# Block transposes on VectorE and a trip through memory in place of TensorE transposes, for batches 4 to 7

## The chip, the cores and the metric

The kernel runs on one core of a Trainium2 chip. The metric is the device time of one execution, in microseconds; lower is better. Three runs of the kernel before gave 366.84, 367.55 and 368.38 us, a median of 367.55.

## What is computed

Eight batches of 512 rows with 512 features pass a gated channel attention over a context and then a gated, quantised feed-forward net (FFN). Only the second half matters here. Cut to that:

```python
def _quant_per_tensor(x):
    scale = max(max(abs(x)), 1e-6) / 127
    return round(x / scale), scale

def _qlinear(x2d, w, b):
    xq, sx = _quant_per_tensor(x2d)
    wq, sw = _quant_per_tensor(w)
    return (xq @ wq.T + b) * (sw * sx)

x = x + tanh(g_xattn) * attention(layernorm(x), ctx)
h = gelu(_qlinear(layernorm(x), w1, b1))       # 512 -> 2048
x = x + tanh(g_ffn) * _qlinear(h, w2, b2)      # 2048 -> 512
```

The scale of `h` is a maximum over all hidden values of all eight batches. So the second product can't begin before the last hidden value of the first is known.

## The kernel before, in words

The rows of a batch lie on 128 partitions, four rows to a partition (`NT` = 4 tiles of 128 rows), and stay in `X` for the whole kernel. The attention runs batch by batch up to about 140 us. From there to about 262 us comes the first FFN product, in eight **groups**, one per batch; after it the hidden values are scaled, rounded and multiplied by the second weights.

One group `g` does this:

- VectorE rounds the batch (`quantise_x`, L1010): four shifts of 128x512 (L1023) write integers into chunk 3 of a ring slot, and one cast (L1027) makes bf16 of them in the first half of chunk 2.
- TensorE turns the rounded rows with sixteen 128x128 transposes (`transposes`, L1389) into the two PSUM banks `psX`, so that features lie on partitions.
- VectorE copies them to `xqT` in `mid` with two copies (`evacuate`, L1033). `mid` has three slots, one for each of the ring's.
- TensorE computes 16 blocks of 128 hidden columns, four matmuls of 128x512 each (L1446), into six PSUM banks in rotation (`H_BANK`). Before each block it waits until ScalarE has emptied the bank (`gelu_done`).
- ScalarE applies GELU to each block (L689) and writes the group's 16 blocks into a slot of `ring`: three slots (`SLOTS`) of four chunks of 2048 columns.
- VectorE takes the maximum of each chunk (`group_max`, L1046; per block for the last two chunks of group 7, L1041).
- SP writes the chunks of groups 0 to 4 to memory (`spill`, L375); groups 5 to 7 stay in the ring.

No scheduler orders this. Each engine runs the groups one after another, and what stands before what is the order in which its `group` function is written. Two waits tie them. At a group's first block ScalarE waits for `hm_done` of `turn * (CH * SLOTS) + 1` (L683): `turn` is the group's number divided by three, so group 3 needs all maxima of groups 0 to 2, and group 6 those of groups 0 to 5. And it waits until the slot's last user is spilled. In VectorE's `group` (L1067) batch `g + 1` is rounded at the start of group `g`, after the last maximum of group `g - 1`, and copied out of PSUM between the second and the third maximum; TensorE does the transposes for it at block 12 of 16. Batches 1 and 2 are prepared elsewhere, amid the work on the second weights.

On GpSimd, the difference `T3` of two blocks of the second weights (L547) waits until the products of groups 0 to 5 are done, and `T2` (L550) until those of group 6 are; both go into slots of `mid` that are free by then.

## Time and profile before

| | |
|---|---|
| median of three runs | 367.55 us |
| the profiled execution | 368.52 us, span 366.7 us |
| busy over the span | TensorE 351.1 us (96%), VectorE 329.7 (90%), ScalarE 284.8 (78%), GpSimd 120.0 (33%) |
| stage of the first FFN product, 140 to 262 us | TensorE 119.81 busy of 122.00, VectorE 111.92, ScalarE 97.55, granted TensorE clock 1.00 |

Busy time is an average over stages. In this stage three engines take turns at being waited for, so it is read from the timelines of each, and from what ended each wait. A row of a timeline gives start, length, engine, line, operation, result and operand, the number of instructions merged, and in brackets the idle time ahead of it with what ended it. Operations of one engine overlap a little, so start-to-start times are shorter than durations. Matmul ends are modelled.

### The profile page before, as it was taken

How to read it: one execution, taken by the hardware profiler on the slowest of the kernel's cores; microseconds unless marked ns; L12 is line 12 of the kernel's file. 1: busy time of each engine (PE TensorE's matmuls, PEld its weight loads, DVE VectorE, ACT ScalarE, POOL GpSimd, SP SyncE). 2: the span in 40 equal slices, each digit the busy share in tenths (PEclk: the TensorE clock that was granted, in tenths of full speed). 3: DMA queues.
4: the chain of work that ended last, by engine and by line, in shares of the span. 5: the costliest groups of instructions: out<-in, count | busy, mean ns of one | idle time of the engine just before them, and what ended most of it. 6: DMA issues, size and time to landing. Idle time of an engine off the chain costs nothing.

```text
span 366.7 us, 6639 instructions
## 1 busy us (share of the span) xinstructions
PE 351.1 (96%) x2403; PEld 242.1 (66%) x2416; DVE 329.7 (90%) x630; ACT 284.8 (78%) x493; POOL 120.0 (33%) x178
## 2 busy tenths in 40 slices
PE   8799989999999989999999999999999999999995
PEld 2755767887886875554535445454548888888884
DVE  3489899999999978999999988987769999999996
ACT  1465879889886975879859988789799999999620
POOL 2544578778779791069000000431000000000000
PEclk9699999999999999999999999999999999999999
DMA  7999978566302463858748760000191999995225
GB/s 225 372 405 403 400 282 268 195 233 224 117 9 108 124 220 132 330 243 331 292 165 343 317 260 0 1 2 0 44 415 58 388 395 425 424 422 228 102 116 229
DMA packets 22963, 84.78 MB, mean 231 GB/s; under 512 B 2129, under 2 KB 11857, under 8 KB 14482
## 3 DMA queue, kind: packets, MB, share of 16 engines
q1 hardware_dynamic: 22272, 83.89, 59.3%
q10 hardware_dynamic: 658, 0.46, 0.5%
q8 instruction: 19, 0.31, 0.3%
q14 instruction: 14, 0.11, 0.1%
HBM read 54.99 MB, written 29.36 MB: 230 GB/s over the span
## 4 chain that ended last, share of the span: by engine, by line
PE 59%; DVE 19%; ACT 9%; POOL 5%; issue 5%; DMA 2%; DVEq 0%; SPq 0%; ACTq 0%; POOLq 0%
PE PS L1491 19%; PE PS L1446 17%; PE PS L1266 7%; DVE hmax L1046 6%; PE PS L1327 6%; ACT ring L709 5%; DVE hmax L839 2%; PE PS L1308 2%; PE PS L1275 2%; DVE ring L1023 2%; PE PS L1287 2%; POOL ring L493 2%; DMA X<-in_x 2%; POOL w1q L495 1%; PE PS L1298 1%
## 5 line engine op out<-in xcount | busy, mean ns | idle before, releaser
L689 ACT ACTIVATE ring<-PS,bias,sc 128x512 f32<-128x512 f32 x128 | 96.4, 784 | 22.4 <-DVE hmax L1046 6.8
L1446 PE MATMUL PS<-mid,w1q 128*128 128x512 bf16 x489 | 108.5, 379 | 1.2 <-ACT ring L689 0.3
L1446 PEld LDWEIGHTS PS<-mid,w1q 128*128 128x128 bf16 x500 | 48.4, 98 | 58.4 <-ACT ring L689 1.5
L1046 DVE TENSOR_REDUCE hmax<-ring 128x1 f32<-128x2048 f32 x30 | 67.5, 2281 | 5.6 <-ACT ring L689 5.6
L709 ACT ACTIVATE ring<-ring,sc 128x2048 int16<-128x2048 f32 x29 | 55.6, 1991 | 0.0
L1491 PE MATMUL PS<-w2q,ring 128*128 128x256 f16 x336 | 39.0, 273 | 0.0
L1174 DVE SCALAR_TENSOR_TENSOR X<-PS,sc,X 128x512 f32<-128x512 f32 x48 | 36.1, 766 | 0.0
L1491 PEld LDWEIGHTS PS<-w2q,ring 128*128 128x128 f16 x336 | 32.9, 98 | 4.0
L1266 PE MATMUL PS<-ring 128*128 128x129 f32 x256 | 33.0, 291 | 0.9 <-ACT ring L612 0.9
L1327 PEld LDWEIGHTS PS<-w2q,ring 128*128 128x128 f32 x256 | 29.2, 192 | 6.7 <-issue 6.7
L1266 PEld LDWEIGHTS PS<-ring 128*128 128x128 f32 x256 | 32.1, 207 | 2.1 <-issue 2.1
L1327 PE MATMUL PS<-w2q,ring 128*128 128x128 f32 x256 | 30.5, 277 | 0.4 <-DVE w2q L879 0.4
L621 ACT ACTIVATE ring<-mid,small 128x128 f32<-128x128 f32 x64 | 24.9, 404 | 4.8 <-DVE small L805 4.8
L1491 PE MATMUL PS<-mid,w1q 128*128 128x256 f16 x224 | 26.7, 273 | 0.3 <-DVE X L1174 0.3
L759 DVE BATCH_NORM_STATS2 small<-X 128x6 f32<-128x512 f32 x32 | 20.0, 682 | 7.0 <-DMA X<-in_x 7.0
L886 DVE SCALAR_TENSOR_TENSOR X<-PS,X 128x512 f32<-128x512 f32 x32 | 21.6, 689 | 3.5 <-PE PS L1327 3.4
L1491 PEld LDWEIGHTS PS<-mid,w1q 128*128 128x128 f16 x224 | 21.7, 98 | 3.4 <-issue 0.9
L612 ACT ACTIVATE ring<-X,small 128x512 f32<-128x512 f32 x28 | 20.7, 819 | 4.0 <-POOL small L449 4.0
L577 ACT ACTIVATE ring<-X,small 128x512 f32<-128x512 f32 x32 | 22.9, 716 | 0.5
L547 POOL TENSOR_TENSOR mid<-w2q 128x2048 f16<-128x2048 f16 x1 | 4.1, 4072 | 55.6 <-PE PS L1446 55.6
L727 ACT ACTIVATE w1q<-ring 128x2048 f16<-128x2048 int16 x7 | 13.3, 1902 | 9.2 <-PE PS L1491 9.2
L1167 DVE TENSOR_TENSOR X<-X,small 128x1024 f32<-128x1024 f32 x16 | 19.8, 1235 | 0.1
(151 smaller groups left out, 591.7 us busy)
## 6 DMA issues: line engine op xcount, KB each, us to landing
spilled_hidden<-ring SPq DMA_DIRECT2D x20, 1024.0 KB, 3.9
ring<-spilled_hidden SPq DMA_DIRECT2D x20, 1024.0 KB, 9.3
ring<-in_ctxT SPq DMA_DIRECT2D x8, 1024.0 KB, 5.5
ring<-in_ctx SPq DMA_DIRECT2D x8, 896.0 KB, 8.2
X<-in_x SPq DMA_DIRECT2D x7, 1024.0 KB, 9.5
out<-X SPq DMA_DIRECT2D x7, 1024.0 KB, 9.9
ring<-in_w1T SPq DMA_DIRECT2D x4, 1024.0 KB, 13.4
ring<-in_w2T SPq DMA_DIRECT2D x8, 512.0 KB, 3.5
```

The lines of the kernel that those rows point to most:

```text
L577: nc.scalar.activation(out[:, i, :], X[:, b, i, :], ACT.Square, bias=nmean[:, t:t + 1], accum_out=ssq[:, t:t + 1]).then_inc(sq_done, 1)
L612: nc.scalar.activation(q_sb[b % 2][:, i].rearrange("p h d -> p (h d)"), X[:, b, i, :], ACT.Identity, scale=rstd1[:, i:i + 1], bias=nmr1[:, ...
L621: nc.scalar.activation(E_sb[:, j, :], S_sb[:, j, :], ACT.Exp, scale=-1.0, bias=nb[:, j:j + 1], accum_out=Z[:, j:j + 1]).then_inc(exp_done, 1)
L689: nc.scalar.activation(ring[:, s * CH + c, (h % CH) * N:(h % CH + 1) * N], PS[:, hidden_bank(s, h), :], ACT.Gelu, scale=SC1, bias=bias1[:, ...
L709: nc.scalar.activation(ring16[:, s * CH + c, 0:CW], ring[:, s * CH + c, :], ACT.Copy, scale=ISH).then_inc(hy_done, n)
L886: V.scalar_tensor_tensor(X[:, b, i, :], PS[:, OUT_BANK[i], :], 1.0, X[:, b, i, :], ALU.mult, ALU.add, accum_out=sums[:, 4 * b + i:4 * b + ...
L1046: V.tensor_reduce(hmax[:, bass.ds(CH * g + c, 1)], ring[:, s * CH + c, :], AX.X, ALU.max, apply_absolute_value=True).then_inc(hm_done, 1)
L1174: V.scalar_tensor_tensor(x, sums_of(p, bank), SC2, x, ALU.mult, ALU.add).then_inc(added, 1)
L1266: mm = nc.tensor.matmul(PS[:, h // 2, h % 2 * (P + 1):h % 2 * (P + 1) + P + 1], q_sb[b % 2][:, i, h, :], k_sb[b % 2][:, i, h // 2, first:f ...
L1327: mm = nc.tensor.matmul(PS[:, OUT_BANK[i], h * P:(h + 1) * P], cT_sb[b % 2][:, h, i, :], M_sb[b % 2][:, h, :], start=False, stop=(h == NH ...
L1446: mm = nc.tensor.matmul(PS[:, hidden_bank(s, h), :], w1v[:, k, h * P:(h + 1) * P], xqT[:, s, k, :], start=(k == 0), stop=(k == NH - 1))
L1491: mm = nc.tensor.matmul(sums_of(p, bank)[:, j], left[:, k, j * P:(j + 1) * P], right[:, k, :], start=(start and k == 0 and (j == 0 or (p, ...
```

## The change

For batches 4 to 7 (`CARRIED` = 4 and up) TensorE's transposes and VectorE's copies from PSUM are gone. VectorE still rounds the rows. Then it turns them within 32x32 blocks, four instructions of 128x512 bf16 into the second half of chunk 2 (`turn_x`). SP writes the 512 KB to memory (`write_rows`) and reads them back with four DMAs, each of which gathers one of four 32-feature groups into its 32 partitions of `mid` (`fetch_rows`). There the columns of a batch no longer lie in one run: TensorE's moving operand is a view in runs of 32 numbers (`turned_block`). For these batches rounding and turning of batch `g + 2` stand in group `g`, between its second and its third maximum, in place of batch `g + 1`'s rounding at the group's start.

```diff
--- before.py
+++ after.py
@@ -46,6 +46,7 @@
     out_v = out.rearrange("b (p i) d -> b p i d", i=NT)
     w1_v = w1T.rearrange("(k p) (a n) -> p k a n", p=P, a=PIECES // NH)
     w2_v = w2T.rearrange("(q k p) n -> q p k n", p=P, q=PIECES)
+    carry = nc.dram_tensor("carried_rows", (B, NT, 32, NT, D), BF16, kind="Internal").ap()
     spill = nc.dram_tensor("spilled_hidden", (SPILLED * CH, P, CW), F32, kind="Internal").ap()
 
     with ExitStack() as es:
@@ -122,6 +123,21 @@
         bpt = mid[:, 1536:2048]
         S_sb = mid[:, 2048:3072].rearrange("p (j e) -> p j e", e=P)
         xqT = mid[:, :].bitcast(BF16).rearrange("p (s k n) -> p s k n", s=SLOTS, k=NH)
+        xqB = mid[:, :].bitcast(BF16).rearrange("p (s t m) -> p s t m", s=SLOTS, t=NT)
+        CARRIED = SLOTS + 1
+
+        def turned_block(g, k):
+
+            return xqB[:, g % SLOTS].rearrange("p t (k i w) -> p k i t w", k=NH, i=NT)[:, k]
+
+        def rounded_rows(g):
+
+            return ring[:, g % SLOTS * CH + 2, 0:CW // 2].bitcast(BF16)
+
+        def turned_rows(g):
+
+            return ring[:, g % SLOTS * CH + 2, CW // 2:CW].bitcast(BF16)
+
         ring16 = ring[:, :, :].bitcast(I16)
         hq = w1q[:, :].bitcast(F16).rearrange("p (c k n) -> p c k n", c=CH, n=N)
         blocks_h = w1q[:, :].bitcast(F16).rearrange("p (c k n) -> p c k n", c=CH, n=HN)
@@ -199,6 +215,9 @@
         w2_step, w2y_done, w2q_done = (sem(n) for n in ("w2_step", "w2y_done", "w2q_done"))
         xs_step, xs_pow, scales = (sem(n) for n in ("xs_step", "xs_pow", "scales"))
         y_done, xq_done, xT_done, xqT_done = (sem(n) for n in ("y_done", "xq_done", "xT_done", "xqT_done"))
+        turned_x = sem("turned_x")
+        written = [sem(f"written{g}") for g in range(B)]
+        moved = [sem(f"moved{g}") for g in range(B)]
         h_done, gelu_done, hm_done = (sem(n) for n in ("h_done", "gelu_done", "hm_done"))
         spilled = [sem(f"spilled{s}") for s in range(SLOTS)]
         back_in = [[sem(f"back_in{s}_{c}") for c in range(CH)] for s in range(SLOTS)]
@@ -369,10 +388,31 @@
                 load_w2(q)
 
 
+            def write_rows(g):
+
+                sp.wait_ge(turned_x, NT * (g - CARRIED + 1))
+                sp.dma_start(carry[g].rearrange("t r a m -> (t r) a m"),
+                             turned_rows(g).rearrange("p (a m) -> p a m", a=NT)).then_inc(written[g], 16)
+
+            def fetch_rows(g):
+
+                sp.wait_ge(written[g], 16)
+                sp.wait_ge(h_done, KH * (g - SLOTS + 1))
+                for a in range(NT):
+                    sp.dma_start(xqB[32 * a:32 * a + 32, g % SLOTS],
+                                 carry[g].rearrange("t r a m -> a r t m")[a]).then_inc(moved[g], 16)
+
             for g in range(SPILLED):
                 for c in range(CH):
                     sp.wait_ge(gelu_done, KH * g + (c + 1) * KH // CH + len(H_BANK))
                     sp.dma_start(spill[g * CH + c], ring[:, (g % SLOTS) * CH + c, :]).then_inc(spilled[g % SLOTS], 16)
+                    if c == 0 and g > 2:
+                        fetch_rows(g + 1)
+                if g >= 2:
+                    write_rows(g + 2)
+            fetch_rows(SPILLED + 1)
+            write_rows(B - 1)
+            fetch_rows(B - 1)
 
             for p in range(B):
                 if p + SLOTS < B:
@@ -1026,6 +1066,14 @@
                 dve.wait_ge(y_done, 4 * g + 4)
                 V.tensor_copy(xq, yt.rearrange("p i d -> p (i d)")).then_inc(xq_done, 4)
 
+            def turn_x(g):
+
+                dve.wait_ge(xq_done, 4 * g)
+                rows = rounded_rows(g).rearrange("p (i k a w) -> p i k a w", i=NT, k=NH, w=32)
+                out = turned_rows(g).rearrange("p (a k i w) -> p i k a w", a=NT, k=NH, w=32)
+                for i in range(NT):
+                    V.transpose(out[:, i], rows[:, i]).then_inc(turned_x, 1)
+
             def evacuate(g, s):
 
                 dve.wait_ge(xT_done, g + 1)
@@ -1065,14 +1113,17 @@
             V.reciprocal(ISW2, SW2).then_inc(w2_step, 1)
 
             def group(g, s, turn, last):
-                if g > 1 and not last:
+                if g == 2:
                     quantise_x(g + 1, (s + 1) % SLOTS, turn + (s + 1) // SLOTS)
                 group_max(g, s, 0)
                 group_max(g, s, 1)
                 if g == 0:
                     evacuate(2, 2)
-                if g > 1 and not last:
+                if g == 2:
                     evacuate(g + 1, (s + 1) % SLOTS)
+                if 2 <= g < B - 2:
+                    quantise_x(g + 2, (s + 2) % SLOTS, turn + (s + 2) // SLOTS)
+                    turn_x(g + 2)
                 group_max(g, s, 2)
                 group_max(g, s, 3)
 
@@ -1435,16 +1486,22 @@
                         pe.wait_ge(xqT_done, 3)
                         pe.wait_ge(w2_step, 5)
                         across(4, W2MAX).then_inc(w2_all, 1)
-                    if h == (KH // 2 if g == 0 else KH // 4 if g == 1 else 3 * KH // 4) and not last:
+                    if h == (KH // 2 if g == 0 else KH // 4 if g == 1 else 3 * KH // 4) and g + 1 < CARRIED:
                         if g == 1:
                             pe.wait_ge(w2_step, 6)
                         transposes(g + 1, (s + 1) % SLOTS)
                     pe.wait_ge(gelu_done, KH * g + h + 1)
                     for k in range(NH):
-                        if h == 0 and k % 2 == 0:
+                        if h == 0 and k % 2 == 0 and g < CARRIED:
                             pe.wait_ge(xqT_done, 2 * g + k // 2)
-                        mm = nc.tensor.matmul(PS[:, hidden_bank(s, h), :], w1v[:, k, h * P:(h + 1) * P], xqT[:, s, k, :],
-                                              start=(k == 0), stop=(k == NH - 1))
+                        if h == 0 and k == 0 and g >= CARRIED:
+                            pe.wait_ge(moved[g], 16 * NT)
+                        hidden, w = PS[:, hidden_bank(s, h), :], w1v[:, k, h * P:(h + 1) * P]
+                        if g < CARRIED:
+                            mm = nc.tensor.matmul(hidden, w, xqT[:, s, k, :], start=(k == 0), stop=(k == NH - 1))
+                        else:
+                            mm = nc.tensor.matmul(hidden.rearrange("p (i t w) -> p i t w", i=NT, t=NT), w, turned_block(g, k),
+                                                  start=(k == 0), stop=(k == NH - 1))
                     mm.then_inc(h_done, 1)
 
             groups(pe, group)
```

VectorE, from the first maximum of group 2 to the end of group 3's, before (L1046 is a maximum, L1033 the copy from PSUM, L1023 and L1027 the rounding):

```order
L1046 TENSOR_REDUCE hmax<-ring 128x1 [waits gelu_done] x2
L1033 COPY mid<-PS 128x1024 [waits xT_done]
L1033 COPY mid<-PS 128x1024
L1046 TENSOR_REDUCE hmax<-ring 128x1 [waits gelu_done] x2
L1023 TENSOR_SCALAR ring<-X,small 128x512 [waits xs_step,hm_done,spilled1]
L1023 TENSOR_SCALAR ring<-X,small 128x512 x3
L1027 CAST ring<-ring 128x2048 [waits y_done]
L1046 TENSOR_REDUCE hmax<-ring 128x1 [waits gelu_done] x2
L1033 COPY mid<-PS 128x1024 [waits xT_done]
L1033 COPY mid<-PS 128x1024
L1046 TENSOR_REDUCE hmax<-ring 128x1 [waits gelu_done] x2
```

and in the same place in the changed kernel (L1094 is a maximum, L1081 the copy, L1063 and L1067 the rounding, L1075 the block transposes):

```order
L1094 TENSOR_REDUCE hmax<-ring 128x1 [waits gelu_done] x2
L1081 COPY mid<-PS 128x1024 [waits xT_done]
L1081 COPY mid<-PS 128x1024
L1063 TENSOR_SCALAR ring<-X,small 128x512 [waits xs_step,hm_done,spilled1]
L1063 TENSOR_SCALAR ring<-X,small 128x512 x3
L1067 CAST ring<-ring 128x2048 [waits y_done]
L1075 STREAM_TRANSPOSE ring<-ring 128x4x4x32 [waits xq_done]
L1075 STREAM_TRANSPOSE ring<-ring 128x4x4x32 x3
L1094 TENSOR_REDUCE hmax<-ring 128x1 [waits gelu_done] x4
```

The rounding of batch 4 has moved from behind group 2's last two maxima to ahead of them, with its block transposes behind it; the maximum rows that follow, two of group 2 and two of group 3, have nothing between them.

TensorE, from the transposes of batch 3 (in group 2) to the end of group 7, before (L1389 transposes, L1446 the product):

```order
L1389 MATMUL PS<-small,ring 128x128 x16
L1446 MATMUL PS<-mid,w1q 128x512 x64
L1389 MATMUL PS<-small,ring 128x128 x16
L1446 MATMUL PS<-mid,w1q 128x512 x64
L1389 MATMUL PS<-small,ring 128x128 x16
L1446 MATMUL PS<-mid,w1q 128x512 x64
L1389 MATMUL PS<-small,ring 128x128 x16
L1446 MATMUL PS<-mid,w1q 128x512 x64
L1389 MATMUL PS<-small,ring 128x128 x16
L1446 MATMUL PS<-mid,w1q 128x512 x80
```

and in the changed kernel (L1440 transposes, L1501 and L1503 the product):

```order
L1440 MATMUL PS<-small,ring 128x128 x16
L1501 MATMUL PS<-mid,w1q 128x512 x80
L1503 MATMUL PS<-mid,w1q 128x512 x256
```

The four later sets of sixteen transposes are gone, and the 256 matmuls of groups 4 to 7 stand in one run, at L1503 with the new operand.

SP, from the first spill to the read of batch 5 in the changed kernel, where before there are twenty spills in a row (L408 is a spill, L394 the write of turned rows, L402 their read):

```order
L408 DMA spilled_hidden<-ring 128x2048 [waits gelu_done] x12
L394 DMA carried_rows<-ring 128x2048 [waits turned_x]
L408 DMA spilled_hidden<-ring 128x2048 [waits gelu_done]
L402 DMA mid<-carried_rows 32x4x512 [waits h_done,written4]
L402 DMA mid<-carried_rows 32x4x512 x3
L408 DMA spilled_hidden<-ring 128x2048 [waits gelu_done] x3
L394 DMA carried_rows<-ring 128x2048 [waits turned_x]
L408 DMA spilled_hidden<-ring 128x2048 [waits gelu_done]
L402 DMA mid<-carried_rows 32x4x512 [waits h_done,written5]
L402 DMA mid<-carried_rows 32x4x512 x3
```

The write of a batch stands behind the last spill of the group in which it was turned, and its read behind the first spill of the next group; batches 6 and 7 follow after the last spill.

## Rows read from the trace of the kernel before

**Rows 1.** Windows of groups 4 and 7 (stretch: length, busy of each engine and count, clock, DMA).

```profile
201.30:216.00 14.70, 14.60 (x80) 7.13 (x80) 12.68 (x11) 12.47 (x16) 0.00 (x0) 1.00 0.71 290
...
245.40:259.00 13.60, 13.55 (x66) 6.47 (x64) 11.04 (x10) 12.25 (x17) 3.41 (x1) 1.00 0.00 0
```

**Rows 2.** Waits in 138 to 262 us: total, times, longest.

```profile
ACT ring L689 <- DVE hmax L1046: 6.8, 2, 4.4
```

**Rows 3.** Timeline of VectorE, groups 2 and 3.

```profile
177.17 1.92 DVE L1023 TENSOR_SCALAR ring<-X,small 128x512 int16<-128x512 f32 x4
179.19 0.69 DVE L1027 CAST ring<-ring 128x2048 bf16<-128x2048 int16 x1
179.80 4.47 DVE L1046 TENSOR_REDUCE hmax<-ring 128x1 f32<-128x2048 f32 x2
...
189.77 1.91 DVE L1023 TENSOR_SCALAR ring<-X,small 128x512 int16<-128x512 f32 x4
...
195.43 2.29 DVE L1046 TENSOR_REDUCE hmax<-ring 128x1 f32<-128x2048 f32 x1 [0.39 <-ACT ring L689]
```

**Rows 4.** Timeline of ScalarE, groups 3 and 6.

```profile
189.94 11.35 ACT L689 ACTIVATE ring<-PS,bias,sc 128x512 f32<-128x512 f32 x16 [4.37 <-DVE hmax L1046]
...
233.11 8.14 ACT L689 ACTIVATE ring<-PS,bias,sc 128x512 f32<-128x512 f32 x12 [2.40 <-DVE hmax L1046]
```

**Rows 5.** Timeline of TensorE, groups 3 to 7, and the product's row of the page.

```profile
185.01 5.43 PE L1446 MATMUL PS<-mid,w1q 128*128 128x512 bf16 x24 [0.26 <-DVE mid L1033]
190.77 5.35 PE L1446 MATMUL PS<-mid,w1q 128*128 128x512 bf16 x23 [0.33 <-ACT ring L689]
...
210.67 1.06 PE L1389 MATMUL PS<-small,ring 128*128 128x128 bf16 x16
...
225.38 1.06 PE L1389 MATMUL PS<-small,ring 128*128 128x128 bf16 x16
...
241.19 17.21 PE L1446 MATMUL PS<-mid,w1q 128*128 128x512 bf16 x78
L1446 PE MATMUL PS<-mid,w1q 128*128 128x512 bf16 x489 | 108.5, 379 | 1.2 <-ACT ring L689 0.3
```

**Rows 6.** Timeline of VectorE, and a row of the page: operations of 512 and 2048 numbers.

```profile
139.93 0.49 DVE L999 CAST mid<-ring 128x512 bf16<-128x512 int16 x2
...
164.01 13.25 DVE L1046 TENSOR_REDUCE hmax<-ring 128x1 f32<-128x2048 f32 x6
...
254.55 3.66 DVE L1041 TENSOR_REDUCE hmax<-ring 128x1 f32<-128x512 f32 x6
L1174 DVE SCALAR_TENSOR_TENSOR X<-PS,sc,X 128x512 f32<-128x512 f32 x48 | 36.1, 766 | 0.0
```

**Rows 7.** Timelines of GpSimd and VectorE at the end of group 5.

```profile
230.04 4.07 POOL L547 TENSOR_TENSOR mid<-w2q 128x2048 f16<-128x2048 f16 x1 [55.63 <-PE PS L1446]
232.94 2.82 DVE L1023 TENSOR_SCALAR ring<-X,small 128x512 int16<-128x512 f32 x4
```

**Rows 8.** DMA issues of the page (count, KB each, us to landing), and SP's timeline.

```profile
spilled_hidden<-ring SPq DMA_DIRECT2D x20, 1024.0 KB, 3.9
...
ring<-in_ctx SPq DMA_DIRECT2D x8, 896.0 KB, 8.2
25.16 0.43 SPq L335 DMA_DIRECT2D ring<-in_w1T  x1
```

**Rows 9.** Windows near the start, and TensorE's timeline there.

```profile
10.00:15.00 5.00, 3.76 (x17) 3.18 (x18) 1.60 (x3) 3.58 (x10) 3.21 (x5) 0.63 1.06 367
15.00:18.00 3.00, 3.00 (x15) 3.00 (x15) 2.16 (x8) 0.00 (x0) 1.10 (x4) 0.50 1.07 401
18.00:20.00 2.00, 2.00 (x9) 0.99 (x10) 1.13 (x3) 0.00 (x0) 1.04 (x2) 0.98 1.01 418
10.38 0.82 PE L1251 MATMUL PS<-w1q 128*128 128x512 bf16 x3 [1.33 <-POOL small L449]
12.06 6.70 PE L1266 MATMUL PS<-ring 128*128 128x129 f32 x32 [0.86 <-ACT ring L612]
```

## The prediction

> **What bounds the kernel now.** I read the page first, then the stage of the first FFN product (140 to 262 us) in windows, then its waits, then the timelines of VectorE, ScalarE and TensorE there. The change touches nothing outside this stage, and what follows it starts from the last maximum of the hidden values, so the question is only when that maximum comes.
>
> In a settled group TensorE and VectorE are both nearly full: of the 14.70 us of group 4, TensorE is busy 14.60 and VectorE 12.68 [rows 1]. TensorE sets the pace: one batch of transposes starts at 210.67 and the next at 225.38, a period of 14.71 us, and the last 80 matmuls without transposes between them (78 are recorded) run from 241.19 in 17.21 us, which is (17.21 - 0.38) / 79 = 0.213 us each [rows 5]. So 64 matmuls are 13.63 us, and 16 transposes cost 14.71 - 13.63 = 1.08 us of TensorE.
>
> VectorE, however, begins this steady part late. ScalarE waits 6.8 us in two places for VectorE's maxima [rows 2]: the ring has three slots, so group 3 may overwrite group 0's only when all maxima of groups 0 to 2 are taken, and group 6 when those of groups 0 to 5 are. At group 3 it waits 4.37 us and starts at 189.94, just when VectorE leaves the last maximum of group 2 (its next operation starts at 189.77) [rows 3, 4]. TensorE feels little of it: from 185.01 it fills the six hidden banks, 24 matmuls, and stands 0.33 us until 190.77 [rows 5]. Thus at this point TensorE's cover is used up: **what VectorE does more before 189.77 is added to the time one for one.** At group 6 ScalarE waits 2.40 us and the banks cover it whole [rows 4].
>
> **The change, part by part.**
>
> *TensorE.* Batches 4 to 7 lose their transposes: 4 x 1.08 = 4.3 us gained, if TensorE is what waits last. Its 256 matmuls now read the moving operand in runs of 32 numbers; no row shows such a read, and a matmul's nearest rows, all with contiguous operands, take 0.213 us. I take no price, since the column count is the same, and keep a slower read as a rival.
>
> *VectorE, per batch.* Two PSUM copies go from each of groups 3 to 6. The rounding of batches 4 to 7 stays: from 177.17 to 179.80, 2.63 us for the four shifts and the cast [rows 3]. Four block transposes of 128x512 bf16 come with it. The first waits for the cast: where the shifts' end at 179.09 releases the cast it starts 0.10 later, where nothing is waited for an operation starts 0.08 before the end of the one ahead (the cast ends at 179.88, the maximum starts at 179.80) [rows 3], so add 0.18. No row shows a VectorE transpose. Bounds: the cast of 128x512 follows itself after 0.49 - 0.29 = 0.20 us; an operation of 512 numbers that also reads PSUM takes 0.75; a reduction of 512 numbers repeats every (3.66 - 0.69) / 5 = 0.594 [rows 6]. I take 0.594, because a transpose must hold a whole block before it gives the first row of it, which looks like the plain one-per-cycle rate and not like the packed copy. A batch is then **W = 2.63 + 0.18 + 4 x 0.594 = 5.19 us** (3.61 and 5.81 at the ends). The Trainium skill (Vector Engine (DVE) Microarchitecture Reference, section 3.8) says the transposing front-end sustains one element per cycle per lane; by its figure and the skill's 0.96 GHz a transpose is at least 512 / 0.96 = 0.533 us, an estimate, which would make W 4.94 and the whole sum below 1.0 us less.
>
> *Where it is put.* Before, batch 4 was rounded after group 2's last maximum. Now the rounding and turning of batch 4 stand ahead of group 2's last two maxima, that is, before the point that releases ScalarE for group 3. That point, S, moves from 189.77 to 189.77 + W. **First stall: +5.19 us** on TensorE (it stands with six full banks from 190.1 to 190.77 + W, some 5.8 us).
>
> *From there to group 6.* TensorE goes on at S + 1.00 (190.77 against 189.77), does 42 hidden columns (10 of group 3, 16 each of 4 and 5) at 4 x 0.213 = 0.852, that is 35.8, and 6 of group 6 at 5.1: it needs ScalarE's release by S + 41.9. VectorE starts group 3's second maximum at S + 5.66 (195.43 against 189.77 before [rows 3]; ScalarE runs at the same rate from its release) and then has no gap: 11 maxima at (13.25 - 2.28) / 5 = 2.19 us [rows 6], 24.1, and three batches of W. All maxima of groups 0 to 5 are done at S + 29.8 + 3W, and TensorE goes on 1.00 later: at S + 30.8 + 3W = S + 46.3. **Second stall: 3W - 11.1 = +4.5 us.** VectorE has per group 4 x 2.19 + 5.19 = 13.95 us against TensorE's 13.63: it no longer catches up what it lost at the start.
>
> *The way through memory.* Each batch is 512 KB out and back, five more issues on SP's queue at about 0.43 us each [rows 8]. SP is in order, so the spills of groups 3 and 4 queue behind waits for VectorE and for the write; ScalarE's next use of a spilled slot is a group or more away. Group 4 is tightest: its read is issued after group 3's first spill, a quarter of ScalarE's 11.35 us after its release [rows 4] or about S + 3.1, the spill's issue and its own four end about S + 5.3, and it lands 3.9 to 8.2 us later (as the spills and the context's loads do [rows 8]), at S + 9.2 to S + 13.5; TensorE wants it at S + 1.0 + 10 x 0.852 = S + 9.5. So it costs 0 to 4.0 us there; for group 5, turned by S + 5.66 + 2.19 + W = S + 13.0 and written 0.4 + 3.9 later, the same sum gives S + 23.0 to S + 27.3 against S + 23.2. But TensorE, late by less than the second stall, only finds that stall shorter, since VectorE's chain doesn't wait for it. I count 0.
>
> *Sum.* W + (3W - 11.1) - 4.3 = **4W - 15.4 = +5.4 us**. The profiled execution took 368.52 us (span 366.7), so 373.9 by it; the median of the three runs is 0.97 lower, and my number is 367.55 + 5.4 = **372.9 us**. At the ends: W = 3.61 leaves no second stall and gives 3.6 - 4.3 = -0.7; W = 5.81 gives +7.8.
>
> **The rivals.**
>
> *A. The block transpose is fast (not slower).* If it runs at the rate of the packed cast, 0.20 us, the second stall is gone, the time is 366.9, no change; the change stays within +1.8 us up to W = 4.3, a transpose of 0.38. Even a transpose for nothing gives 2.8 - 4.3 = -1.5 us, because the rounding was moved ahead of S. For it: casts of the same type do run so. Against: reductions, statistics and two-input operations of 512 numbers all take about 0.6 or more. Chance 0.10.
>
> *B. VectorE and GpSimd meet.* The sum of B22 and B12 on GpSimd starts when group 5's products end and takes 4.07 us. Before, it ran from 230.04 beside maxima; one shift of VectorE, begun at 232.94 while it still ran, made the four shifts 2.82 us where they are 1.92 [rows 3, 7]. Now group 5's products end at S + 36.8, and VectorE rounds batch 7 from S + 5.66 + 9 x 2.19 + 2W = S + 35.7 to S + 38.4: GpSimd asks in the middle of it. If it gets in between two operations, the rest waits out its 4.07 us, about 3.9 us more before all of group 6: 376.8 us. Against: the row shows only VectorE waiting for a GpSimd operation that already ran, not GpSimd coming between back-to-back ones; and if TensorE is late by more than 1.5 us at group 4 or 5 the two no longer meet. Chance 0.20.
>
> *C. TensorE's clock falls in the stalls.* It is at 1.00 all through this stage [rows 1]. Near the start it was granted 0.63 in 10 to 15 us and 0.50, the lower level (1.2 GHz), in 15 to 18, after TensorE had stood 1.33 and 0.86 us between a few matmuls; at 18 to 20 it was back at 0.98 [rows 9]. That is 3.7 + 3.0 = 6.7 us at half speed, 3.35 us lost. After the first stall such a loss disappears into the second; after the second it stays: 376.3 us. The Trainium skill (TensorE: Matmul & The Clock Gate, section Why this matters for your kernels) warns that an idle gap between bursts of matmuls brings the lower clock back; both stalls here would be such gaps, the longest of the stage. Chance 0.15.
>
> *D. Something else costs more:* short runs that slow TensorE's read, or the return trip late by more than the second stall hides: 377 to 385 us. Chance 0.07.
>
> **How the numbers follow.** The forecast, two stalls and no more, has 0.45, and its own range is 371 to 375.4 (transposes of 0.48 to 0.75). The range reaches over B and C, 376.8 and 376.3, and a little over their sum with a W of 0.3 more: 370 to 379 us; left out are most of A and part of D. About 0.5%, 1.8 us, is what a measurement of this kernel can tell from no change. Faster than that needs a gain that no row shows me, 0.03; within it is A, 0.10; the forecast, B, C and D are slower, 0.87.
>
> **What would show it.** In the profile after: ScalarE's wait for maxima grows from 4.4 to 9 to 10 us at group 3 and from 2.4 to about 8 at group 6; TensorE has two gaps of some 5.5 and 4.3 us, at group 3 and group 6, and none between groups 4 and 5 longer than the landing sum allows; block transposes of about 0.6 us apiece in start-to-start time; the last hidden maximum about 5 us later, and the stage after it unchanged. A transpose below 0.4 us, or a VectorE that waits for ScalarE in groups 4 and 5, would make the prediction wrong; so would a matmul step other than 0.213 us in groups 4 to 7.

## The result and the profile after

The changed kernel takes **374.12 us** (372.94 to 374.47, four runs), the kernel before in the same comparison 367.37 (366.84 to 368.38): a ratio of 1.0173, interval 1.0153 to 1.0194. Forecast were 372.9 us and a range of 370 to 379. The profiled execution took 374.47 us with a span of 370.9; so 3.6 us lie outside the span, where before it was 1.8.

First ScalarE. Its waits for maxima, which were 6.8 us in two [rows 2], in the view of waits (total, times, longest):

```profile
ACT ring L729 <- DVE hmax L1094: 14.6, 2, 9.5
```

The two of them in ScalarE's timeline, which answers to [rows 4]:

```profile
193.50 5.46 ACT L729 ACTIVATE ring<-PS,bias,sc 128x512 f32<-128x512 f32 x8 [9.48 <-DVE hmax L1094]
...
239.15 24.27 ACT L729 ACTIVATE ring<-PS,bias,sc 128x512 f32<-128x512 f32 x32 [5.09 <-DVE hmax L1094]
```

The wait at group 3 has grown from 4.37 to 9.48 us, at group 6 from 2.40 to 5.09. VectorE's timeline shows what it does in the first of them; L1063 and L1067 round, L1075 turns, L1094 is a maximum (it answers to [rows 3]).

```profile
183.82 1.91 DVE L1063 TENSOR_SCALAR ring<-X,small 128x512 int16<-128x512 f32 x4
185.83 0.69 DVE L1067 CAST ring<-ring 128x2048 bf16<-128x2048 int16 x1
186.56 2.49 DVE L1075 STREAM_TRANSPOSE ring<-ring 128x512 bf16<-128x512 bf16 x4
188.98 4.44 DVE L1094 TENSOR_REDUCE hmax<-ring 128x1 f32<-128x2048 f32 x2
...
213.37 2.29 DVE L1094 TENSOR_REDUCE hmax<-ring 128x1 f32<-128x2048 f32 x1 [0.40 <-ACT ring L729]
...
229.47 1.91 DVE L1063 TENSOR_SCALAR ring<-X,small 128x512 int16<-128x512 f32 x4
231.48 0.70 DVE L1067 CAST ring<-ring 128x2048 bf16<-128x2048 int16 x1
232.21 2.49 DVE L1075 STREAM_TRANSPOSE ring<-ring 128x512 bf16<-128x512 bf16 x4
234.63 4.44 DVE L1094 TENSOR_REDUCE hmax<-ring 128x1 f32<-128x2048 f32 x2
```

The page's row of the block transposes (busy us, mean ns of one, idle before):

```profile
L1075 DVE STREAM_TRANSPOSE ring<-ring 128x512 bf16<-128x512 bf16 x16 | 10.0, 679 | 0.1
```

A batch takes VectorE from 183.82 to 188.98, **W = 5.16 us**, and that stands ahead of the two maxima that release ScalarE at 193.42. This is the point S of the prediction. The 24th maximum ends at 234.63 + 4.44 = 239.07, S + 45.65; behind group 3's second maximum VectorE waits once on this way, 0.40 us for ScalarE in group 4.

TensorE's timeline (it answers to [rows 5]; L1501 and L1503 are the product, L1297 is the first work after the stage):

```profile
183.46 5.43 PE L1501 MATMUL PS<-mid,w1q 128*128 128x512 bf16 x24 [0.25 <-DVE mid L1081]
194.33 11.29 PE L1501 MATMUL PS<-mid,w1q 128*128 128x512 bf16 x40 [5.44 <-ACT ring L729]
205.45 32.97 PE L1503 MATMUL PS<-mid,w1q 128*128 128x512 bf16 x152
239.98 22.62 PE L1503 MATMUL PS<-mid,w1q 128*128 128x512 bf16 x104 [1.56 <-ACT ring L729]
262.44 0.83 PE L1297 MATMUL PS<-ident 128*128 128x128 f32 x6
```

The first gap is there, 5.44 us. The second is only 1.56 where 4.3 was named. Between them 40 matmuls took 11.12 us (194.33 to 205.45), though each of the 104 at the end takes (22.62 - 0.38) / 103 = 0.2159, and 40 of those are 8.64. The windows around the first gap (stretch: length, busy of TensorE, its weight loads, VectorE, ScalarE and GpSimd, each with its count, then the granted clock, the DMA share and GB/s) say why:

```profile
190.00:193.00 3.00, 0.00 (x0) 0.00 (x0) 3.00 (x2) 0.00 (x0) 0.00 (x0) 0.93 0.39 157
193.00:196.00 3.00, 1.67 (x4) 0.58 (x5) 0.41 (x1) 2.50 (x4) 0.00 (x0) 0.50 0.00 0
196.00:198.00 2.00, 2.00 (x6) 0.76 (x5) 1.69 (x1) 2.00 (x4) 0.00 (x0) 0.50 0.48 197
198.00:200.00 2.00, 2.00 (x7) 0.75 (x6) 1.61 (x2) 1.34 (x3) 0.00 (x0) 0.65 1.11 328
200.00:203.00 3.00, 3.00 (x16) 1.37 (x14) 3.00 (x5) 2.72 (x4) 0.00 (x0) 1.00 0.99 282
```

TensorE stands idle, its granted clock goes to 0.50 (1.2 GHz), and only from 200 on does it have 1.00 (2.4 GHz) again. That lost 2.5 us. TensorE so reached the second stall 2.5 us later and stood there for less time; run 3 shows how much of the loss the stall took in. The Trainium skill (TensorE: Matmul & The Clock Gate, section Why this matters for your kernels) warns of idle gaps between bursts; the trace agrees, with 0.50 after 5.44 us of idleness.

**TensorE's account.** From the start of the x24 row to the first matmul behind the stage, TensorE needed 258.24 - 185.01 = 73.23 us before and 262.44 - 183.46 = 78.98 after, 5.75 more. The account takes that apart by start-to-start times, a matmul at 0.2158:

- first stall: 183.46 to 194.33 less 24 matmuls is 5.69, before it was 0.58 (185.01 to 190.77): **+5.11**;
- clock: 11.12 less 40 matmuls: **+2.49**;
- second stall: 205.45 to 239.98 less 152 matmuls: **+1.73**;
- transposes no longer done: a batch of them and 64 matmuls took 14.71 [rows 5], less 13.81 is 0.90, four times: **-3.6**.

The sum is +5.73 of 5.75. Behind the stage nothing has changed: both executions take 108.46 us from there to the end of the span (366.7 less 258.24, 370.9 less 262.44).

The medians lie 6.75 apart, 1.0 more; the four runs reach from +5.6 to +7.1. The account can't say where the rest lies, but the record has two hints that it is scatter. Ahead of the stage, where the code is the same, the two profiled executions differ by 1.55 us (185.01 against 183.46). And the two executions that make the median of the change have spans of 372.0 and 372.1 us at a mean granted clock of 0.981, where the profiled one has 370.9 at 0.985. No trace of one of them is kept, so this stays open.

### The profile page after: what moved, and what is told of

It is laid out like the page before. It is cut to its first block, busy times and chain, and to the rows that moved or that the text cites. A ratio compares the mean times of both kernels' runs of the same rounds, so it can differ in the third digit from the quotient of the medians.

```text
span 370.9 us, 6552 instructions
## 1 busy us (share of the span) xinstructions
PE 349.9 (94%) x2352; PEld 237.8 (64%) x2352; DVE 333.7 (90%) x638; ACT 284.4 (77%) x493; POOL 119.8 (32%) x178
## 4 chain that ended last, share of the span: by engine, by line
PE 51%; DVE 27%; ACT 9%; POOL 5%; issue 5%; DMA 1%; DVEq 0%; SPq 0%; ACTq 0%; POOLq 0%
PE PS L1548 19%; DVE hmax L1094 10%; PE PS L1503 8%; PE PS L1317 6%; PE PS L1378 6%; ACT ring L749 5%; PE PS L1501 3%; DVE ring L1063 3%; DVE hmax L879 2%; PE PS L1359 2%; DVE ring L1075 2%; PE PS L1326 2%; PE PS L1338 2%; POOL ring L533 2%; DMA X<-in_x 1%
## 5 line engine op out<-in xcount | busy, mean ns | idle before, releaser
L1094 DVE TENSOR_REDUCE hmax<-ring 128x1 f32<-128x2048 f32 x30 | 67.1, 2274 | 9.7 <-ACT ring L729 9.7
L1501 PE MATMUL PS<-mid,w1q 128*128 128x512 bf16 x244 | 56.3, 391 | 5.7 <-ACT ring L729 5.4
L1503 PE MATMUL PS<-mid,w1q 128*128 128x512 bf16 x256 | 55.6, 379 | 1.6 <-ACT ring L729 1.6
L1501 PEld LDWEIGHTS PS<-mid,w1q 128*128 128x128 bf16 x244 | 24.1, 100 | 36.1 <-ACT ring L729 7.2
L1503 PEld LDWEIGHTS PS<-mid,w1q 128*128 128x128 bf16 x256 | 25.0, 98 | 32.0 <-ACT ring L729 2.1
L1225 DVE SCALAR_TENSOR_TENSOR X<-PS,sc,X 128x512 f32<-128x512 f32 x48 | 35.2, 745 | 0.0
L1317 PE MATMUL PS<-ring 128*128 128x129 f32 x256 | 31.6, 283 | 0.9 <-ACT ring L652 0.9
L1317 PEld LDWEIGHTS PS<-ring 128*128 128x128 f32 x256 | 30.7, 200 | 2.2 <-issue 2.2
```

The source lines that it names most:

```text
L1094: V.tensor_reduce(hmax[:, bass.ds(CH * g + c, 1)], ring[:, s * CH + c, :], AX.X, ALU.max, apply_absolute_value=True).then_inc(hm_done, 1)
L1225: V.scalar_tensor_tensor(x, sums_of(p, bank), SC2, x, ALU.mult, ALU.add).then_inc(added, 1)
L1317: mm = nc.tensor.matmul(PS[:, h // 2, h % 2 * (P + 1):h % 2 * (P + 1) + P + 1], q_sb[b % 2][:, i, h, :], k_sb[b % 2][:, i, h // 2, first:f ...
L1501: mm = nc.tensor.matmul(hidden, w, xqT[:, s, k, :], start=(k == 0), stop=(k == NH - 1))
L1503: mm = nc.tensor.matmul(hidden.rearrange("p (i t w) -> p i t w", i=NT, t=NT), w, turned_block(g, k), start=(k == 0), stop=(k == NH - 1))
```

## The experiments

Each run is compared with runs of the kernel before on the same chip (medians 366.99 to 367.38). The expectations were on record before each run. The same account is drawn up for all of them in a table behind them.

**1. No turning.** VectorE's block transposes are left out, the rest stays.

```diff
-                             turned_rows(g).rearrange("p (a m) -> p a m", a=NT)).then_inc(written[g], 16)
+                             rounded_rows(g).rearrange("p (a m) -> p a m", a=NT)).then_inc(written[g], 16)
...
                     quantise_x(g + 2, (s + 2) % SLOTS, turn + (s + 2) // SLOTS)
-                    turn_x(g + 2)
```

> The sixteen block transposes are left out: the rounded rows of batches 4 to 7 are written to memory unturned and read back by the same DMAs, and TensorE reads the same view of them. Theory (the work put ahead of the maxima sets the time): VectorE's work per batch falls from W = 5.16 us (183.82 to 188.98 in the changed kernel's profile) to the rounding alone, 2.63. The first stall shrinks with it, 3W - 11.1 is below nothing, so there is no second stall, and the time is 367.4 + 2.6 - 4.3 = 365.7 us, some 0.5 more for the matmul step, which now looks like 0.2158 instead of 0.213: 366.2 us, ScalarE waiting about 7 us at group 3 and at most 2.4 at group 6. Rival (the trip through memory, or TensorE's read in short runs, costs the time): both stay, so it remains above 372 us.

Measured: 368.11 us, ratio 1.0018 (1.0003 to 1.0033). ScalarE waits 6.97 at group 3 and 2.50 at group 6, and TensorE's second stall is gone: with W = 2.61 instead of 5.16 the 256 matmuls run in one piece. So the second stall does hang on W. But the time is 1.9 above what was expected. TensorE's timeline:

```profile
191.69 10.21 PE L1500 MATMUL PS<-mid,w1q 128*128 128x512 bf16 x39 [2.94 <-ACT ring L729]
201.73 55.42 PE L1502 MATMUL PS<-mid,w1q 128*128 128x512 bf16 x256
```

The window behind its gap (columns as above):

```profile
192.00:195.00 3.00, 3.00 (x9) 1.11 (x8) 1.33 (x1) 3.00 (x6) 0.00 (x0) 0.57 0.21 87
```

The clock fell after this stall too (10.04 us for 40 matmuls, 1.41 lost), and here no second stall follows that could take it in.

**2. The same with TensorE kept busy.** Twelve matmuls that nobody reads fill the stall.

```diff
+                    if g == 3 and h == len(H_BANK):
+                        for _ in range(12):
+                            nc.tensor.matmul(PS[:, 4, :], w1q[:, 0:P], w1q[:, 0:N], start=True, stop=True)
```

> As in the run without block transposes (they are left out, so the rows of batches 4 to 7 are unturned), but with twelve idle matmuls on a free bank in TensorE's stall at block 6 of group 3, so that its clock has no gap to fall in. Without them the 40 matmuls after the stall were 1.4 to 1.7 us longer than at full clock, and no second stall followed that could hide it. Theory: 367.4 + 2.6 - 4 x 0.90 = 366.4 us, the 0.90 being the 16 transposes by the step of 0.2158. Rival (the clock costs nothing there): 368.1 us, as without the idle matmuls.

Measured: 366.60 us, ratio 0.9977 (0.9964 to 0.9989). The 40 matmuls take 8.81 again. So in run 1 the clock cost 1.5 us.

**3. The changed kernel with TensorE kept busy in the first stall** (22 such matmuls, the block transposes in place).

> Twenty-two idle matmuls on a free bank fill TensorE's first stall, at block 6 of group 3. In the changed kernel the granted clock fell to 0.50 from about 193 to 199 us, and the 40 matmuls after the stall took 11.29 us where 8.9 would do: 2.4 us lost. Theory (VectorE's chain sets group 6, so what TensorE loses between the stalls disappears in the second): the clock stays at 1.00, the second stall grows by about 2.4 us, and the time stays at 374.1 us within 0.7. Rival (the clock is part of the price): 371.7 us.

Measured: 373.65 us, ratio 1.0168 (1.0147 to 1.0188), the time that the theory had. Without the clock's loss TensorE isn't done sooner, since the second stall waits for VectorE all the same:

```profile
194.39 8.81 PE L1504 MATMUL PS<-mid,w1q 128*128 128x512 bf16 x39 [0.70 <-ACT ring L729]
203.83 32.97 PE L1506 MATMUL PS<-mid,w1q 128*128 128x512 bf16 x152 [0.63 <-ACT ring L729]
239.56 24.31 PE L1506 MATMUL PS<-mid,w1q 128*128 128x512 bf16 x104 [2.76 <-ACT ring L729]
```

ScalarE's release of group 6, and VectorE's last maxima ahead of it:

```profile
238.73 12.14 ACT L729 ACTIVATE ring<-PS,bias,sc 128x512 f32<-128x512 f32 x16 [6.29 <-DVE hmax L1094]
234.20 4.44 DVE L1094 TENSOR_REDUCE hmax<-ring 128x1 f32<-128x2048 f32 x2
```

From the x24 row to group 6's release on TensorE (the x104 row) it takes 239.56 - 183.52 = 56.04 us, in the changed kernel 239.98 - 183.46 = 56.52. So of the 2.49 us only 0.48 were won, nearly all because VectorE no longer waits in group 4; 0.81 went into a wait ahead of group 4, 1.20 into the second stall. (The row ahead of group 4 names ScalarE, but of its sixteen blocks of group 3, from 193.56 to 204.38, TensorE needed only the eleventh there, done by about 201; what is left to wait for is batch 4's rows from memory.) And now the clock fell behind the second stall: the 104 matmuls took 24.31 us, 1.7 more than in the changed kernel. So the second half of the theory, a second stall longer by 2.4 us and a clock that stays at 1.00, did not come true, and the equal times are in part luck: the stage is 1.2 us longer here.

**4. Batch 4 later.** Batch 4's rounding and turning stand behind group 2's last maximum, as its rounding did before the change.

```diff
-                if 2 <= g < B - 2:
+                if 2 < g < B - 2:
                     quantise_x(g + 2, (s + 2) % SLOTS, turn + (s + 2) // SLOTS)
                     turn_x(g + 2)
                 group_max(g, s, 2)
                 group_max(g, s, 3)
+                if g == 2:
+                    quantise_x(g + 2, (s + 2) % SLOTS, turn + (s + 2) // SLOTS)
+                    turn_x(g + 2)
```

> Only the place of batch 4 is changed: its rounding and turning stand behind group 2's last maximum instead of ahead of the last two. All work is the same. Theory: the first stall is gone; in its place TensorE waits at group 4 for the trip through memory (turned 5.2 us after the release, written 4.2 later, read 4.8 to 6.2 later still, so about 14 to 15.6 us after it, wanted after 9.5), and VectorE's chain ends group 5's maxima 47.5 to 48.7 us after that release instead of 50.8. The time is 371 to 372 us. Rival 1 (only the sum of VectorE's work counts): 374 us. Rival 2 (the trip is what costs): slower than 374 us, since batch 4 comes later.

Measured: 371.09 us, ratio 1.0095 (1.0074 to 1.0117).

```profile
189.66 8.81 PE L1504 MATMUL PS<-mid,w1q 128*128 128x512 bf16 x39 [0.33 <-ACT ring L729]
202.44 34.65 PE L1506 MATMUL PS<-mid,w1q 128*128 128x512 bf16 x152 [3.97 <-DMA mid<-carried_rows]
238.65 22.62 PE L1506 MATMUL PS<-mid,w1q 128*128 128x512 bf16 x104 [1.55 <-ACT ring L729]
```

The first stall is as small as before the change, 0.33 us: it does come from the place of batch 4's work ahead of S. Now batch 4 arrives from memory 3.97 us late, the clock falls there (34.65 against 32.97), and the second gap is as long as in the changed kernel.

**5. No trip through memory.** The writes and reads are left out; TensorE takes what lies in the slots, once VectorE has turned the batch.

```diff
-                    if c == 0 and g > 2:
-                        fetch_rows(g + 1)
-                if g >= 2:
-                    write_rows(g + 2)
-            fetch_rows(SPILLED + 1)
-            write_rows(B - 1)
-            fetch_rows(B - 1)
...
+                if g >= CARRIED:
+                    act.wait_ge(turned_x, NT * (g - CARRIED + 1))
```

> The writes and reads of the turned rows are left out, and TensorE's wait for them: it multiplies what lies in the slots, and ScalarE waits for the block transposes of its group instead, which are done long before. VectorE's work and its order stay. Theory (VectorE's chain to group 3 and to group 6 is the price): 373.4 to 374.8 us, the same two waits of ScalarE for maxima. Rival (the trip, its bandwidth or SP's queue costs something): below 372.5 us.

Measured: 373.10 us, ratio 1.0149 (1.0132 to 1.0166), a little below the band. The account of this run is 0.3 above that of the changed kernel, so by the two profiled executions the 1.0 us between their medians isn't in this stage. The trip costs the changed kernel nothing that its trace shows: writes land after 3.9 us and reads after 3.1 (the page's rows below: count, KB each, us to landing), and TensorE has no gap before groups 4 and 5. In part the clock hides it there: in run 3, at full clock, TensorE stood 0.81 us ahead of group 4.

```profile
carried_rows<-ring SPq DMA_DIRECT2D x4, 512.0 KB, 3.9
mid<-carried_rows SPq DMA_DIRECT2D x16, 128.0 KB, 3.1
```

**6. GpSimd rounds batches 4 to 7**, in four shifts and one operation that adds and takes away a large constant; VectorE only turns.

```diff
+                for i in range(NT):
+                    nc.gpsimd.tensor_scalar(y[:, i * D:(i + 1) * D], X[:, g, i, :], nmean[:, 4 * g + i:4 * g + i + 1],
+                                            rstd[:, 4 * g + i:4 * g + i + 1], ALU.add, ALU.mult).then_inc(y_done, 1)
+                pool.wait_ge(y_done, 4 * g + 4)
+                nc.gpsimd.tensor_scalar(rounded_rows(g), y, MAGIC, -MAGIC, ALU.add, ALU.add).then_inc(xq_done, 4)
...
                 if 2 <= g < B - 2:
-                    quantise_x(g + 2, (s + 2) % SLOTS, turn + (s + 2) // SLOTS)
                     turn_x(g + 2)
```

> GpSimd, idle from 175 to 230 us, rounds batches 4 to 7 in VectorE's place, with the same numbers as a result; VectorE keeps the block transposes where they are. Theory: W is the four transposes alone, 2.43 us, so 367.4 + 2.4 - 4.3 + 0.5 = 366.0 us with no second stall; GpSimd needs about 4 x 0.76 + 1.9 = 4.9 us for a batch and has 13.7. Rival 1 (memory trip or read): stays above 372 us. Rival 2 (GpSimd and VectorE block each other): VectorE's block transposes or maxima become longer than 0.67 and 2.28 us, and the time lies between 368 and 374 us.

Measured: 384.67 us, ratio 1.0475 (1.0447 to 1.0503), a plain miss. GpSimd's timeline:

```profile
195.86 3.03 POOL L593 TENSOR_SCALAR ring<-X,small 128x512 f32<-128x512 f32 x4 [7.04 <-DVE hmax L1110]
199.05 7.09 POOL L596 TENSOR_SCALAR ring<-ring 128x2048 bf16<-128x2048 f32 x1 [0.16 <-POOL ring L593]
```

The last operation takes 7.09 us; it had been taken at the 1.90 of GpSimd's other operations of that size. VectorE waits for it 20.4 us in four places, and two long stalls follow on TensorE. The run says nothing of the theory, only what this form costs.

**7. GpSimd rounds in three steps**, multiply-add and add-multiply in place of add-add, and the turning stands between the third and the fourth maximum.

```diff
+                nc.gpsimd.tensor_scalar(y, y, 1.0, MAGIC, ALU.mult, ALU.add).then_inc(lifted, 1)
+                pool.wait_ge(lifted, g - CARRIED + 1)
+                nc.gpsimd.tensor_scalar(rounded_rows(g), y, -MAGIC, 1.0, ALU.add, ALU.mult).then_inc(xq_done, 4)
...
+                group_max(g, s, 2)
                 if 2 <= g < B - 2:
-                    quantise_x(g + 2, (s + 2) % SLOTS, turn + (s + 2) // SLOTS)
                     turn_x(g + 2)
-                group_max(g, s, 2)
                 group_max(g, s, 3)
```

> GpSimd rounds batches 4 to 7 in three steps of the kinds that it used for the weights (3.0 + 2.0 + 1.9 = 6.9 us for a batch, where the two-step form took 10.2), and VectorE's block transposes stand between the third and the fourth maximum of a group, where GpSimd is done. Theory: ahead of the release of group 3 stand 2.4 us more, the four transposes; group 6 waits at most 1 us; 367.4 + 2.4 - 3.6 = 366.2 us, up to 2 us more by the clock and the second wait: 366.2 to 368.2 us. Rival (GpSimd's operations hold up VectorE's, or GpSimd is late again): VectorE waits for GpSimd by more than 1 us a group, and the time is over 369 us.

Measured: 368.15 us, ratio 1.0016 (1.0002 to 1.0031). Only the turning of batch 4 is left ahead of S: first stall 2.4 us, no second one, and the clock takes 1.7 (10.33 us from 192.10 to 202.43 for 40 matmuls).

```profile
192.10 3.32 PE L1518 MATMUL PS<-mid,w1q 128*128 128x512 bf16 x10 [2.70 <-ACT ring L747]
195.64 6.95 PE L1518 MATMUL PS<-mid,w1q 128*128 128x512 bf16 x29 [0.22 <-issue]
202.43 55.57 PE L1520 MATMUL PS<-mid,w1q 128*128 128x512 bf16 x256
```

**8. Three batches carried.** As run 7, but batch 4 stays with TensorE, so nothing is put ahead of S.

```diff
-        CARRIED = SLOTS + 1
+        CARRIED = SLOTS + 2
...
```

The places that went by batch 4's number, of the reads and writes and of VectorE's rounding and turning, follow it.

> The same with batches 5 to 7 alone: batch 4 is rounded, transposed on TensorE and copied as before, so nothing stands ahead of the release of group 3 that did not stand there before. GpSimd rounds 5 to 7 in three steps, VectorE turns them between the third and the fourth maximum. Theory: no first stall beyond that of before, no second (group 6's release comes 43.2 us after group 3's, TensorE wants it at 43.0), and three sets of transposes saved: 367.4 - 3 x 0.90 + 0.2 = 364.9 us, faster than both. Rival 1 (GpSimd and VectorE block each other): 366 to 369 us. Rival 2 (the trip costs): TensorE waits at group 5, 6 or 7 for the rows, 366 us or more.

Measured: 364.53 us (364.19 to 365.70), ratio 0.9921 (0.9907 to 0.9935), **below both kernels**.

```profile
183.27 5.43 PE L1518 MATMUL PS<-mid,w1q 128*128 128x512 bf16 x24 [0.25 <-DVE mid L1099]
189.03 5.35 PE L1518 MATMUL PS<-mid,w1q 128*128 128x512 bf16 x23 [0.33 <-ACT ring L747]
194.22 1.06 PE L1457 MATMUL PS<-small,ring 128*128 128x128 bf16 x16
195.11 17.43 PE L1518 MATMUL PS<-mid,w1q 128*128 128x512 bf16 x78
212.38 41.76 PE L1520 MATMUL PS<-mid,w1q 128*128 128x512 bf16 x192
```

TensorE runs from group 4 to the end without a gap, and VectorE waits for ScalarE in every group.

**9. The same rounding on GpSimd, with TensorE's transposes.** The kernel before with only the rounding of batches 5 to 7 moved: does run 8 gain by the transposes or by a relieved VectorE?

> The kernel before, with GpSimd rounding batches 5 to 7 in three steps as in the last run, but with TensorE's transposes and VectorE's two copies kept. If the last run's gain comes from the three sets of transposes that TensorE no longer does (3 x 0.90 = 2.7 us), nothing is gained here: TensorE sets the pace and only VectorE has less to do, so 367.4 (366.8 to 368.0). If it comes from VectorE being relieved, this kernel gains as much: 364.5.

Measured: 367.42 us, ratio 1.0006 (0.9991 to 1.0020). Relieving VectorE alone gives nothing; run 8's gain is the three sets of transposes.

```profile
239.04 1.06 PE L1409 MATMUL PS<-small,ring 128*128 128x128 bf16 x16
239.94 17.43 PE L1466 MATMUL PS<-mid,w1q 128*128 128x512 bf16 x80
```

Sixteen transposes take 239.94 - 239.04 = 0.90 us from start to start.

**10. The same turning and trip, with the rounding on VectorE**, between the third and the fourth maximum.

> Batch 4 as in the kernel before, batches 5 to 7 through memory, VectorE rounding and turning each of them between the third and fourth maximum. Nothing is put ahead of the release for group 3, so no first stall. VectorE from S: rounding of batch 4 and the second maximum to S + 5.66 + 2.19, two copies 1.2, ten maxima of 2.19 and three W of 5.16: the 24th maximum ends at S + 46.4, TensorE can go on at S + 47.4 and needs it by S + 1.0 + 42 x 0.863 + 0.9 + 5.2 = S + 43.3. A second stall of 4.1 us, less 3 x 0.90 = 2.7: 367.4 + 1.4 = 368.8, and 370.3 if TensorE's clock falls in it as in the run without turning. If the order alone were at fault (the rounding and turning ahead of the release of group 3) and not the amount of VectorE's work, this kernel would gain the transposes: 364.7.

Measured: 373.81 us, ratio 1.0181 (1.0150 to 1.0212), another miss: 3.5 above the higher of the two numbers. There is no first stall, but the second is 6.9 us:

```profile
239.13 24.48 PE L1503 MATMUL PS<-mid,w1q 128*128 128x512 bf16 x104 [6.73 <-ACT ring L729]
```

VectorE's timeline at the rounding of batch 7:

```profile
227.16 5.56 DVE L1063 TENSOR_SCALAR ring<-X,small 128x512 int16<-128x512 f32 x4
```

GpSimd's timeline there:

```profile
227.02 4.05 POOL L587 TENSOR_TENSOR mid<-w2q 128x2048 f16<-128x2048 f16 x1 [54.26 <-PE PS L1503]
```

All 28 shifts of the kernel, by line (shortest, median and longest duration in ns):

```profile
L1063 DVE TENSOR_SCALAR ring<-X,small x28: 535/543/4189, 140.8 to 232.2; 128x512 int16<-128x512 f32 x28
```

This is the meeting of the prediction's rival B. GpSimd's sum begins 0.14 us before the shifts, the first of which takes 4.19 us instead of 0.54, 3.65 more: it ends at 231.35, and the sum at 231.07. The Trainium skill (SBUF — State Buffer, section SBUF: two separate sides) says that GpSimd and some VectorE operations, those in a two-port mode or with two SBUF inputs, share one pair of ports as an exclusive lock: whichever starts first has it for the whole instruction. The trace agrees, with a shift that waits out GpSimd's operation; which mode a shift runs in no view shows. With the clock's 1.9 us in the stall behind it the sum is 367.0 + 1.4 + 3.65 + 1.9 = 373.9.

**11. GpSimd's sum put behind batch 7's turning**, all else as in run 10.

```diff
             pool.wait_ge(h_done, KH * (B - 2))
+            pool.wait_ge(turned_x, NT * (B - CARRIED))
             nc.gpsimd.tensor_tensor(T3, B22, B12, ALU.subtract).then_inc(weight_sums, 1)
```

> As the last run (batches 5 to 7 through memory, VectorE rounding and turning), but GpSimd begins the sum of B22 and B12 only when VectorE has turned batch 7. If the meeting of the two is what made the four shifts of batch 7 take 5.56 us instead of 1.91, they take 1.91 again, the 24th maximum ends at S + 46.4, TensorE's gap falls from 6.7 to about 3.1 us, and the time by 3.6 us to 370.2 (369.6 to 370.9). If those shifts are slow for another reason (their place in the program, the DMAs at that time), nothing changes: 373.8.

Measured: 369.88 us (368.32 to 371.47), ratio 1.0063 (1.0042 to 1.0084). The four shifts take 1.92 us and TensorE's gap is 3.57.

```profile
227.28 1.92 DVE L1064 TENSOR_SCALAR ring<-X,small 128x512 int16<-128x512 f32 x4
235.60 24.31 PE L1504 MATMUL PS<-mid,w1q 128*128 128x512 bf16 x104 [3.57 <-ACT ring L730]
```

Against the kernel before on its own chip run 10 is 6.82 us slower and this run 2.58, so the meeting cost run 10 about 4.2 us. In the stage it is 3.8 (table below): 3.15 in the second stall, 0.5 in waits for rows and 0.2 by the clock.

**The account of all runs**, drawn up as above, in us against the kernel before. "Other gaps" are those at the arrival of rows from memory and small ones. "Stage" is the measured difference from the x24 row to the first matmul behind the stage, "median" that of the run times.

| run | first stall | clock | other gaps | second stall | transposes | sum | stage | median |
|---|---|---|---|---|---|---|---|---|
| the change | 5.11 | 2.49 | 0 | 1.73 | -3.6 | 5.73 | 5.75 | 6.75 |
| 1 no turning | 2.62 | 1.41 | 0 | 0 | -3.6 | 0.43 | 0.45 | 0.78 |
| 2 and busy | 2.61 | 0 | 0.67 | 0 | -3.6 | -0.32 | -0.31 | -0.78 |
| 3 busy | 5.11 | 1.70 | 0.81 | 2.93 | -3.6 | 6.95 | 6.95 | 6.32 |
| 4 batch 4 later | 0 | 1.68 | 4.15 | 1.73 | -3.6 | 3.96 | 3.96 | 3.76 |
| 5 no trip | 5.12 | 2.69 | 0 | 1.81 | -3.6 | 6.02 | 6.04 | 5.72 |
| 6 GpSimd, add-add | 7.40 | 4.16 | 1.24 | 8.40 | -3.6 | 17.60 | 17.60 | 17.34 |
| 7 three steps | 2.37 | 1.70 | 0.16 | 0 | -3.6 | 0.63 | 0.63 | 0.77 |
| 8 three carried | 0 | 0 | 0.16 | 0 | -2.7 | -2.54 | -2.53 | -2.85 |
| 9 GpSimd, TensorE | 0 | 0 | 0 | 0 | 0 | 0 | -0.01 | 0.43 |
| 10 VectorE, memory | 0 | 1.88 | 0.78 | 6.89 | -2.7 | 6.85 | 6.85 | 6.82 |
| 11 sum later | 0 | 1.71 | 0.28 | 3.74 | -2.7 | 3.03 | 3.03 | 2.58 |

The sum meets every stage to within 0.03 us, but its gaps and clock losses are cut from the same start times as the stage, so this only shows that no matmul time is left over: one step and one price for a set of transposes fit all twelve kernels. The medians are the independent check: within 0.65, except that of the change itself (1.0).

## Why the prediction was right, point by point

- **W and the first stall: right.** 5.16 us against 5.19. A block transpose follows the one ahead after (2.49 - 0.67) / 3 = 0.607 us, where 0.594 was taken from the reductions. By the prediction's estimate from the Trainium skill (Vector Engine (DVE) Microarchitecture Reference, section 3.8) it would have been 0.533, at one element per cycle; the measurement is 0.07 us above it. Runs 1, 4 and 8 show that the stall follows what stands ahead of S: 2.6 us with the rounding alone, none with nothing; in run 7 it is 2.4 with the turning alone.
- **The second stall: right in mechanism, too large in size.** 4.5 us were forecast. In run 3, where the clock doesn't fall ahead of it, the 24th maximum ends at 238.64, S + 45.16 (forecast S + 45.3), and TensorE stands 0.81 + 2.93 = 3.74 us. In the changed kernel clock and second stall together took 2.49 + 1.73 = 4.22. So two of the prediction's signs, a second gap of some 4.3 us and a wait of ScalarE of about 8, came out at 1.56 and 5.09. A third, a VectorE that waits for ScalarE in groups 4 and 5, came up with 0.40 us in group 4 and made the 24th maximum S + 45.65. The fallen clock is behind the third and part of the other two: in run 3 VectorE has no such wait in group 4, ScalarE's wait at group 6 is 6.29 us and the second gap 2.76. What is left of the gap is the 0.81 us ahead of group 4 and the slip of the next point. Runs 1 and 7, with a small W, have no second stall.
- **Transposes: the mis-sized term.** The prediction divided 17.21 us by 79, but only 78 of those 80 matmuls are recorded, and the row begins after the first of them, so it holds 78 steps. The step is 0.2158 in both kernels (run 9's unbroken row: (17.43 - 0.38) / 79), so sixteen transposes cost 0.90 us and not 1.08, and the change saves 3.6 instead of 4.3. The same slip lets TensorE want group 6's release 0.55 us too early and made the second stall that much too large. One error is against the change and one for it, so the sum is off by little: that is luck. With the measured terms at full clock it is 5.11 + 3.74 - 3.6 = +5.25, and the 0.48 that the clock cost makes +5.73, where +5.4 was forecast. The remaining 1.0 us of the median is outside this account and stays open.
- **The read in runs of 32 and the trip: rightly counted at nothing.** The step is 0.2158 with either operand, so the sign of a step other than 0.213 is the prediction's slip and not a slower read. The trip is hidden in the changed kernel; at full clock in run 3 it cost 0.81 us ahead of group 4, within the 0 to 4.0 named, and the second stall was shorter for it. In run 4, where batch 4 was turned later, it cost 4.15 us.
- **Rival C: its mechanism came true, in the place where by its own words it costs nothing.** The clock fell in the first stall, and all but 0.48 us of its 2.49 vanished ahead of group 6. Run 2 shows the price where no second stall follows (1.5 us). Behind the second stall, where the rival says that the loss stays, the clock fell in run 3 (a gap of 2.76 us, 1.70 lost) and not in the changed kernel, whose gap was only 1.56.
- **Rival B: did not happen, by little.** In the changed kernel GpSimd's sum started at 233.39, after the shifts of batch 7 (229.47 to 231.38), because TensorE was late, mostly by the clock. In run 3, without that loss, it started 0.8 us after the shifts' end; without TensorE's 0.81 us ahead of group 4 it would have started about as they end. Both came by the prediction's exception, a late TensorE. The two rows are GpSimd's in the changed kernel and in run 3:

```profile
233.39 4.07 POOL L587 TENSOR_TENSOR mid<-w2q 128x2048 f16<-128x2048 f16 x1 [60.55 <-PE PS L1503]
231.77 4.07 POOL L587 TENSOR_TENSOR mid<-w2q 128x2048 f16<-128x2048 f16 x1 [58.85 <-PE PS L1506]
```

  The price given, 3.9 us, is near what run 10 paid (3.65 on VectorE, 3.8 in the stage and 4.2 in run time by run 11). The prediction's case against it, that GpSimd doesn't come between back-to-back operations, was never tested, since in run 10 GpSimd came first.
- **Rivals A and D: no.** The transposes follow each other after 0.61 us, not 0.20, and no read or trip was late by more than the second stall hides.

## What to carry to other kernels

Before moving work to an engine that has idle time, find the operation on it that releases others, and put the work behind it: the same rounding and turning added 5.1 us to the first stall ahead of that point and nothing to it behind (run 4), though the batch then came 4 us late; what is moved must also be done before its result is wanted. Where an engine has no slack per period, lateness adds up from period to period (3W here) until the next shared buffer collects it, so an offload must also fit the period of the engine that takes it; here that needed a third engine (runs 8 to 11: 364.5 us with GpSimd rounding, 373.8 and 369.9 with VectorE, 367.4 with the transposes left on TensorE). And a loss ahead of a later stall can be free: price it by what comes after, not by itself.
